# Four equal-unit expert batches with gated result gathers, in a graph and mixture-of-experts kernel

## What is computed

```python
msg = layernorm(x) @ W + B
weights = where(adj < 1, exp(-(1/adj - 1)**2 / 0.5), 0)
x = x + weights @ msg
z = layernorm(x)
vals, idx = top_k(z @ gate_w + gate_b, 2)
share = softmax(vals)
expert_out[e] = relu(z @ w1[e] + b1[e]) @ w2[e] + b2[e]
y = z + sum_k share[k] * expert_out[idx[k]]
out = x + layernorm(y) * gamma + beta
```

## Time and profile before

| | us |
|---|---|
| median of three runs | 1702.58 (1701.91 to 1702.87) |
| profiled execution, its span | 1823.2 |
| PE busy in it | 1624.7 (89%) |
| ACT busy | 1565.7 (86%) |
| DVE busy | 1499.7 (82%) |
| POOL busy | 463.6 (25%) |

### The profile page before, as it was taken

How to read it: one execution, slowest core, us unless ns; L and a number is a source line. 1 busy time by engine, 2 the same in 40 slices (tenths; PEclk the granted TensorE clock), 3 DMA queues, 4 the chain that set the end, 5 groups by cost and what they waited for, 6 DMA issues and landing times.

```text
span 1823.2 us, 24195 instructions
## 1 busy us (share of the span) xinstructions
PE 1624.7 (89%) x8178; PEld 1073.6 (59%) x8178; DVE 1499.7 (82%) x2298; ACT 1565.7 (86%) x1502; POOL 463.6 (25%) x342
## 2 busy tenths in 40 slices
PE   4999999999999999999999999999999987384720
PEld 3666666666666666666666656666666786373620
DVE  7999998989899999999999989999998443153464
ACT  5899999999999999999999999999999664253531
POOL 0001223131314040407132231313140213535342
PEclk9999999999999999999999999999999999696765
DMA  9559867676767676776776676787673244343431
GB/s 313 158 160 290 235 199 215 195 217 193 214 195 212 196 212 198 220 213 202 210 202 209 199 210 199 209 247 208 202 206 121 80 124 143 87 141 97 129 110 50
DMA packets 216792, 338.22 MB, mean 186 GB/s; under 512 B 18080, under 2 KB 74144, under 8 KB 216544
## 3 DMA queue, kind: packets, MB, share of 16 engines
q1 hardware_dynamic: 208368, 319.62, 59.8%
q0 software_dynamic: 8304, 17.06, 3.1%
HBM read 303.07 MB, written 33.55 MB: 185 GB/s over the span
## 4 chain that ended last, share of the span: by engine, by line
PE 84%; DVE 6%; another core or an unknown queue 5%; issue 3%; ACT 1%; DMA 1%; DVEq 0%; SPq 0%; ACTq 0%
PE acc L1118 48%; PE tp L1137 24%; PE tp L1164 4%; PE tp L1192 3%; PE acc L1192 2%; DVE chunk L654 1%; PE tp L1153 1%; DVE stats L666 1%; DVE chunk L660 1%; DVE chunk L1004 1%; PE misc L1094 1%; ACT chunk L613 1%; DVE msg L729 1%; DMA xs<-in_x_dram 1%
## 5 line engine op out<-in xcount | busy, mean ns | idle before, releaser
L1118 PE MATMUL acc<-wT,msg 128*128 128x512 f32 x2048 | 976.0, 599 | 0.0
L527 ACT ACTIVATE wT<-tp 128x1024 f32<-128x1024 f32 x512 | 761.0, 1674 | 14.0 <-PE tp L1137 12.4
L521 ACT ACTIVATE chunk<-chunk 128x2048 f32<-128x2048 f32 x256 | 655.3, 2560 | 0.1
L660 DVE SCALAR_TENSOR_TENSOR chunk<-chunk 128x2048 f32<-128x2048 f32 x256 | 584.8, 2284 | 54.7 <-ACT chunk L521 54.1
L1137 PEld LDWEIGHTS tp<-ident,chunk 128*128 128x128 f32 x4096 | 478.7, 141 | 223.2 <-issue 221.5
L654 DVE SCALAR_TENSOR_TENSOR chunk<-chunk 128x2048 f32<-128x2048 f32 x256 | 583.5, 2280 | 1.9 <-DMA chunk<-in_adj_dram 1.9
L1137 PE MATMUL tp<-ident,chunk 128*128 128x128 f32 x4096 | 534.3, 274 | 0.0
L516 ACT ACTIVATE chunk<-chunk 128x4096 f32<-128x4096 f32 x118 | 511.0, 4331 | 0.0
L1118 PEld LDWEIGHTS acc<-wT,msg 128*128 128x128 f32 x2048 | 349.1, 190 | 258.3 <-issue 245.8
L457 POOL TENSOR_TENSOR pool_carrier<-pool_carrier 1x1 f32<-1x1 f32 x32 | 43.7, 1365 | 951.5 <-DVE row_now L845 825.9
L476 POOL DMA_INDIRECT rows_in<-y,row_now x128 | 216.7, 1693 | 40.4 <-issue 40.4
(11 more groups left out here) (121 smaller groups left out, 794.7 us busy)
## 6 DMA issues: line engine op xcount, KB each, us to landing
chunk<-in_adj_dram SPq DMA_DIRECT2D x256, 1024.0 KB, 5.4
chunk<-rows_in SPq DMA_DIRECT2D x118, 64.0 KB
rows_out<-chunk SPq DMA_DIRECT2D x59, 128.0 KB
chunk<-rows_in SPq DMA_DIRECT2D x35, 128.0 KB
rows_out<-chunk SPq DMA_DIRECT2D x17, 256.0 KB
y_kept<-y SPq DMA_DIRECT2D x16, 256.0 KB, 6.1
chunk<-y_kept SPq DMA_DIRECT2D x16, 256.0 KB
out_dram<-chunk SPq DMA_DIRECT2D x16, 256.0 KB
```

The costliest lines, as they stand in the source:

```text
L521: act.activation(slot(c), slot(c), ACT.Exp, scale=-1.0).then_inc(inverted, 1)
L527: act.activation(wT[:, (g * PPG + m) % WSLOTS, :], tp[(g * PPG + m) % TSLOTS][:, :], ACT.Exp, scale=-2.0).then_inc(weighted, 1)
L660: dve.scalar_tensor_tensor(out=slot(c), in0=slot(c), scalar=2.0, in1=slot(c), op0=ALU.subtract, op1=ALU.mult).then_inc(squared, 1)
L1118: ins = pe.matmul(acc[:, :], msg[:, n, :], wT[:, (g * PPG + m) % WSLOTS, k * ROWS:(k + 1) * ROWS], start=(n == 0), stop=(n == 2 * PPG - 1))
```

## The change

Two constants and the planning of gathers and combines are changed. The batches are 3, 5, 5 and 3 groups, all in units of one tile: 39, 55, 55 and 39 units, again 188 tiles. Each single gather now has a gate: a count of finished units (`ro_ready`) that GpSimd waits for. A running tile number t goes up by 1.8 for each gather, and is at least the tile at which the batch ends plus 4; the gate is the number of units that end before tile t. Gathers for which t would be beyond the last tile have no gate. A combine begins 4 tiles after the last gather of its group, and at least 11 slots after the one before: slots 60, 74, 89, 115, 129, 144, 158, 173, 187, 198, 209, 220, 231, 242, 253, 264. Slots from 188 on have no units. The gates are for group 0 units 43 to 56, for group 3 units 98 to 111, for group 8 units 171 to 183, and for the first two gathers of group 9 units 185 and 187; the other 54 gathers have none.

```diff
-    BATCHES = (7, 5, 4)
-    TILES = (1, 2, 1)
+    BATCHES = (3, 5, 5, 3)
+    TILES = (1, 1, 1, 1)
...
-        COMBINE_WAIT, COMBINE_PACE, COMBINE_LONG = 8, 6, 11
-        starts = []
+        COMBINE_LONG, LOAD_Z_AHEAD = 11, 6
+        GATHER_PACE, RESULTS_LATE, LANDED = 1.8, 4, 4
+        tiles_done = [0]
+        for u in range(NU):
+            tiles_done.append(tiles_done[-1] + TILES[batch_of(u)])
+        def units_at(t):
+            return sum(d < t for d in tiles_done)
+        gather_after, starts = {}, []
+        t = 0
         for b, n in enumerate(BATCHES):
-            for _ in range(n):
-                at = UNIT0[b + 1] + COMBINE_WAIT
-                pace = COMBINE_PACE if starts and UR[batch_of(starts[-1])] > P else COMBINE_LONG
-                starts.append(max(at, starts[-1] + pace) if starts else at)
+            for g in range(FIRST[b], FIRST[b + 1]):
+                for kb in range(KB):
+                    t = max(t + GATHER_PACE, tiles_done[UNIT0[b + 1]] + RESULTS_LATE)
+                    if t <= tiles_done[-1]:
+                        gather_after[g, kb] = units_at(t)
+                at = units_at(t + LANDED)
+                starts.append(max(at, starts[-1] + COMBINE_LONG) if starts else at)
...
-                    if i == starts[g] - COMBINE_PACE:
+                    if i == starts[g] - LOAD_Z_AHEAD:
...
                     for kb in range(KB):
+                        if (g, kb) in gather_after:
+                            pool.wait_ge(ro_ready, gather_after[g, kb])
                         pool.indirect_dma_start(
```

## The result

The changed kernel takes **1758.6 us** (1758.41 to 1759.72), the kernel before 1702.7 (1701.91 to 1705.54): a ratio of 1.0327, 95% interval 1.0312 to 1.0341. It is 56 us slower. The forecast was 1741 in a range of 1703 to 1765, so the sign and the range held, but the difference is 1.44 times the 38.7 us of the sum. The profiled span had been forecast at 1770 to 1840 and is 1756.9; that forecast missed.

A forecast was written before the change was run, and what follows sets the result against it. It took TensorE to bound the graph stage and set the unit pace. After: 1436.05 + 200.4 + 12.0 + 12.6 + 83.5 = 1744.6, less 1705.9 before, +38.7 on the 1702.6 median: 1741 us, range 1703 to 1765.

The forecast's parts named there:

- the sum: Whole kernel: 1705.9 us before, 1744.6 after, so +38.7 us, on the median 1741; chance 0.53.
- The end: Behind the last result: 55 gathers take 71.1 us, then landing, last combine and store, 83.5 us against 61.5.
- The first combine: At slot 60 VectorE waits for gathers queued behind the last group's scatters: +12.6 us (8 to 17).
- The units: Expert units after: 200.4 us for 188 tiles against 194.8, combines 12.0 against 13.5, plus the 12.6 us wait.
- Part 1: All units of one tile: TensorE +5.6 us; VectorE's extra work costs nothing, 0.97 us of 1.17 a unit.
- B: Rival: bursts of gathers stall the units in unrecorded runs too; the gates take away 66 us: 1675, chance 0.12.
- C: Rival: gates leave combines no slack; gathers come 2.9 us late in each of eight, +23: 1764, chance 0.14.
- D: Rival: an unrecorded gather costs 0.95 us without the 0.31 gap; end 69.5 rather than 83.5: 1722, chance 0.16.
- E: Rival: gates are passed before GpSimd reaches them, spreading nothing; held only for the first 24 gathers; no separate chance.
- Signs: VectorE waiting 12 us, 54 or 55 gathers at the end, 2 us waits a group, units at 1.07 and 1.2.
- the floor of 1685.6 us: Kernel before, every tile at 1.0 us and combines free: 1436 + 188 + 61.5, leaving at most 17 us of stall.
- The reason beside it: Stalls in the first profiled execution: the whole 117 us would come from recording the trace.

The follow-up runs named there:

- experiment 2: The changed kernel without the gates of single gathers, the combines keeping their slots: 1744.3 us, ratio 1.0238 to the kernel before.
- experiment 3: The changed kernel with its first combine 13 slots later and one gather per 1.3 tiles instead of 1.8: 1725.0 us.
- experiment 4: The changed kernel's gates and plan of combines with the batches and unit widths of the kernel before: 1736.7 us.
- experiment 1: The changed kernel with its first combine 13 slots later, nothing else changed: 1741.5 us.
- experiment 5: The kernel of experiment 3 with its two middle batches in units of two tiles and combines 6 slots apart there: 1726.3 us.
- `COMBINE_WAIT` 10: The kernel before with each batch's first combine two slots later (10 for 8): 1703.3 us, ratio 0.9997.
- `COMBINE_LONG` 8: The kernel before with combines among narrow units and behind the last unit 8 slots apart instead of 11: 1711.0 us.

## Why the prediction was right, and where its sum was off

**The end: right.** 83.0 us for 83.5 forecast, against 62.2 for 61.5. 54 gathers at 1.29 us bind it, not the combines. Experiments 2, 3 and 4 moved the number of gathers left (24, 37, 65) and the end followed: 61.4 us for 37, 100.0 for 65; with 24 the combines bind, as they do in the kernel before.

**The first combine: right, but priced too low.** 12.06 us of wait for 12.6. Removing it gave 17.1 (some of that from other waits, as experiment 1 says). The step that was too small is "+12.6 us (8 to 17)": it priced the wait alone and left out the half clock behind it, though the earlier trace rows showed a clock of 0.57 in a stretch in which TensorE had little to do.

**The units: the term that was mis-sized.** The sum gave them 225.0 us after and 208.3 before, and they took 237.3 and 203.5. The 12.3 us too few for after and the 4.9 too many for before both made the forecast difference too small.

For the kernel after, the prices of a unit and of a combine are not what failed. Its units 41 to 59, without combines, take 18.25 us, 1.01 each, under the 1.066 of the prediction; that came from units 0 to 47 of before. The last batch of before, with four combines one behind the other, takes 53.15 us from unit 106 to 152, or 1.155 each. That is 0.14 more a slot, some 1.6 us a combine, against 1.5. What failed is that the sum had nothing for stops other than the first wait: the half clock (some 7 us, an estimate), the wait for y (2.85), and the batch boundary at unit 39. From unit 30 to 41 both kernels run the same program but for that boundary, in 12.09 us before and 15.14 after, so it costs 3.1. With the first wait 0.5 shorter than forecast that is 12.4 of the 12.3 missing; the agreement is closer than the estimate for the clock deserves.

For the kernel before, the sum charged 7.5 us for five combines among wide units that are free: the middle batch takes 70.6 us, 69.1 of them 35 x 1.975 (the pace in the earlier trace rows is 1.973), and has a wait of 3.7 us in it. So the middle batch was charged 76.5 us for 70.6. The last was charged 56.1 for 53.2, and the first 75.7 for 79.7, and the sum of before came out 4.7 us over its span of 1701.2. I read the 3.3 us over the median as agreement, and that was luck. Part 1 called the cover "0.97 together, of 1.17": busy time under the pace. It says nothing of what a single long wait does: in these runs wide units absorbed waits of up to 3.7 us nearly whole, and narrow ones didn't.

Of the 33.8 us of the units, experiment 1 places 18.4 with the first combine (the half clock behind it and behind the wait for y among it), and 3.1 are the boundary at unit 39. The rest, 12 us, no run isolates. About half of it I put down to combines, an estimate: before, five of nine are among wide units and free; after, eight whole ones are among narrow units at 1.6 us. The half clock that is left in experiment 1 is worth 3 more.

**Rivals.** B (bursts stall the units) fell with experiment 2. C (each combine waits for its last gather) fell: among the units only three of nine combines waited for gathers, 12.1, 1.2 and 0.3 us. D (a gather is cheaper unrecorded) fell, since a profiled execution takes the timed runs' time. E had the gates passed before GpSimd comes to them for the first 24 gathers. The trace shows ten such gathers, back to back from 1503.84 on; from the eleventh, at 1516.92, GpSimd waits at its gates, since VectorE and with it the units had stopped. For the first wait only group 0 matters, so the sum doesn't change by it.

**Signs.** The prediction's list came true in the wait of 12 us, the 54 gathers at the end, and VectorE's wait for them (13.7 us for seven combines, 2 a group). The paces were lower than listed: 1.01 us for 1.07 alone, and 1.11 for 1.2 with combines (units 97 to 148, 56.7 us).

**A right conclusion from a wrong reason.** That the stalls of the profiled execution are not in the timed runs held; it followed from the floor of 1685.6 us. The reason beside it did not hold: the same recording leaves an execution without stalls. By the Trainium skill, NOTIFIC — the notification-queue block, section 7.1, that block holds its producers back inside rather than lose a record; nothing of that shows in these runs, 1701.2 us of span in 1702.9. Nor does what the Trainium skill says of GpSimd's DMAs beside VectorE's fp32 copies (SBUF — State Buffer, "SBUF: two separate sides"), that their descriptors can't be written meanwhile: the median gather took 0.94 to 0.95 us among the units and behind them, in both kernels.

**Gates and plan against batches and units.** The plan alone costs 34 us (experiment 4), 38 more at the end and 4 less in the units. The batches and narrow units on top of it cost 22: the units take 38 us more (237.3 for 199.1), of which 18 are the first combine at slot 60 instead of 82 and 3 the boundary, while the end is 17 us shorter, since 54 gathers are left instead of 65.

## What to carry to other kernels

Before pacing a transfer, count what will be left when the work that it hides under ends: gates can only delay, and here each gather pushed behind the last unit cost 1.29 us once gathers and not combines bound the end, while bursts of them among the units stopped nothing. Price a step that lies "beside other work" for each kind of that work separately: the same combine was free beside wide units, cost 1.6 us beside narrow ones eleven slots apart, and 4.7 when the kernel before had them eight slots apart (9.4 us for two more). Price a wait with what it leaves behind: here TensorE's half clock, also after waits of only 3 us, and only where the units had no slack. And when one profiled execution disagrees with the timed runs, take a second one before explaining the first.

## What the runs showed of the hardware

After a wait of 12 us TensorE came back at 1.2 GHz and reached 2.4 GHz again about 5.5 us later; the matmuls of a unit took 1.06 us in between instead of 0.61. In the kernel after the clock was halved after idle times of 3.86 and 2.47 us too. The kernels whose middle units are wide, in experiments 4 and 5, before the change, and with `COMBINE_WAIT` 10, show no such stretch among their units; the one with `COMBINE_LONG` 8 shows it only among its last, narrow units (from 1635 on).

Reading a table of up to sixteen values into VectorE's registers is not small. This is the row of the kernel after (duration in ns, min/median/max):

```profile
L989 DVEq TENSOR_LOAD <-e_tab x14: 539/1250/2854, 1445.1 to 1652.4; - x14
```

Each batch boundary adds one on VectorE, TensorE and SyncE, which is what I take the 3.1 us at unit 39 to be; no run isolates it.

One execution of the kernel before was 120 us longer than all others, with TensorE, VectorE and ScalarE held up at once during bursts of gathers, while GpSimd went on issuing (15.4 us of 20 busy). It did not come again in any of the executions shown here.
